# Two-layer attention kernel: the coarse score pieces of layer 0 by row halves of TensorE's array, and the softmax denominators as rows that VectorE inverts in PSUM

## The reference

```
layer 0:  theta, phi, g = W x + b       (64 rows each)
          f = softmax(theta^T phi);   y = f g;   x = W_out y + b_out + x
layer 1:  q, k, v = W x + b             (128 rows each)
          a = softmax(q^T k / sqrt(128));   x = x + v a^T
```

## Time and profile before

| | before |
|---|---|
| median of 3 runs | 3435.5 us |
| profiled execution, its own time | 3435.51 us |
| its span | 3433.7 us |
| granted clock, mean over the span | 0.989 |
| block of layer 0 (steady) | 44.03 us |
| block of layer 1 (steady) | 59.9 us |

### The profile page before, as it was taken

How to read it: one execution, slowest core, us unless ns; L and a number is a source line. 1 busy time by engine, 2 the same in 40 slices (tenths; PEclk the granted TensorE clock), 3 DMA queues, 4 the chain that set the end, 5 groups by cost and what they waited for, 6 DMA issues and landing times.

```text
span 3433.7 us, 46684 instructions
## 1 busy us (share of the span) xinstructions
PE 3336.5 (97%) x13124; PEld 2113.4 (62%) x13124; DVE 2100.6 (61%) x3029; ACT 1671.5 (49%) x2241; POOL 2965.9 (86%) x1366
## 2 busy tenths in 40 slices
PE   6999999999999989999999998999999999999998
PEld 4555566666655556666655555666665555566665
DVE  4555576776555557676755555677675555666674
ACT  4455445444455544444445554544454555444444
POOL 4999699898989969898989996989898999688897
PEclk9999999999999999999999999999999999999999
DMA  1000000000000000000000000000000000000000
GB/s 43 13 18 19 28 10 22 12 22 16 19 19 16 19 23 16 16 19 19 13 19 19 19 16 23 19 13 21 16 19 13 19 19 16 19 13 16 13 13 10
DMA packets 34038, 61.73 MB, mean 18 GB/s; under 512 B 5280, under 2 KB 5920, under 8 KB 33568
## 3 DMA queue, kind: packets, MB, share of 16 engines
q1 hardware_dynamic: 33824, 59.23, 5.6%
HBM read 42.44 MB, written 16.78 MB: 17 GB/s over the span
## 4 chain that ended last, share of the span: by engine, by line
PE 91%; DVE 3%; issue 2%; POOL 2%; ACT 1%; SPq 0%; DVEq 0%; DMA 0%; ACTq 0%; POOLq 0%
PE acc_out L471 16%; PE rough L398 15%; PE acc_out L455 13%; PE scores L420 7%; PE scores L423 7%; PE scores L425 7%; PE scores L429 7%; PE scores L426 7%; PE acc_out L443 2%; PE acc_out L441 2%; PE acc_out L442 2%; DVE piece_max L793 2%; PE rough L380 2%; PE acc_out L492 1%; PE acc_out L386 1%
## 5 line engine op out<-in xcount | busy, mean ns | idle before, releaser
L280 POOL TENSOR_TENSOR sums<-sums,probs 128x1024 f32<-128x1024 f32 x886 | 2116.0, 2388 | 145.1 <-ACT probs L718 104.7
L793 DVE TENSOR_REDUCE piece_max<-rough 128x1 f32<-128x512 f32 x2024 | 1309.5, 684 | 649.1 <-PE rough L398 646.2
L810 DVE TENSOR_TENSOR probs<-scores,shift_rows 128x1024 f32<-128x1024 f32 x512 | 626.7, 1224 | 567.3 <-PE scores L429 543.2
L718 ACT ACTIVATE probs<-scores 128x1024 f32<-128x1024 f32 x512 | 520.1, 1025 | 672.8 <-PE scores L423 665.1
L711 ACT ACTIVATE probs<-probs 128x1024 f32<-128x1024 f32 x512 | 539.4, 1053 | 499.6 <-DVE probs L810 499.4
L914 POOL TENSOR_TENSOR p_lo<-probs,p_hi 128x1024 fp32r<-128x1024 f32 x192 | 459.2, 2392 | 188.0 <-ACT probs L711 187.7
L471 PE MATMUL acc_out<-probs,v_vals 128*128 128x512 f32 x1280 | 605.4, 595 | 0.0
L425 PE MATMUL scores<-qry_a,k_hi 128*128 128x512 f32 x1024 | 507.8, 496 | 0.0
L455 PE MATMUL acc_out<-probs,g_vals 128*64 128x512 f32 x2048 | 495.0, 605 | 0.0
L420 PE MATMUL scores<-qry_a,phi_a 128*128 128x512 f32 x1024 | 432.3, 422 | 0.0
L710 ACT ACTIVATE p_hi<-probs 128x1024 fp32r<-128x1024 f32 x192 | 203.3, 1059 | 441.0 <-DVE probs L810 397.2
(11 more groups left out here) (97 smaller groups left out, 2961.0 us busy)
## 6 DMA issues: line engine op xcount, KB each, us to landing
x_q<-x SPq DMA_DIRECT2D x32, 256.0 KB, 2.7
x_res<-x SPq DMA_DIRECT2D x32, 256.0 KB, 3.0
mid<-mid_new SPq DMA_DIRECT2D x32, 256.0 KB, 2.2
x_q<-mid SPq DMA_DIRECT2D x32, 256.0 KB, 2.7
x_res<-mid SPq DMA_DIRECT2D x32, 256.0 KB, 3.2
out<-result SPq DMA_DIRECT2D x32, 256.0 KB, 2.3
x_kv<-x SPq DMA_DIRECT2D x24, 256.0 KB, 2.7
probs<-x SPq DMA_DIRECT2D x2, 1024.0 KB, 6.0
```

What stands on the lines that cost most here:

```text
L280: eng.tensor_tensor(sums[:, parity], sums[:, parity], probs[:, s % P_BUFS], ALU.add).then_inc(s_plus, 1)
L793: nc.vector.reduce_max(piece_max[:, t, c:c + 1], src, AX.X).then_inc(s_reduced, 1)
L810: nc.vector.tensor_tensor(probs[:, s % P_BUFS].rearrange("p (h c) -> p h c", c=QB), scores[:, s % 2].rearrange("p (h c) -> p h c", c=QB), ...
```

## The change

```diff
 DEN_AT = 5
-RDEN_AT = 8
+RECIP_AT = (6, 7, 8, 9)
+NORM_AT = 9
...
             def rough_piece(layer, parity, piece, place):
                 t, c = piece
-                keys = (phi_a, k_hi)[layer]
-                mm(place, qry_a[:, parity, t * P:(t + 1) * P], cols(keys, c), start=True, stop=True).then_inc(s_rough, 1)
+                at = slice(t * P, (t + 1) * P)
+                if layer == 1:
+                    mm(place, qry_a[:, parity, at], cols(k_hi, c), start=True, stop=True).then_inc(s_rough, 1)
+                elif t % 2 == 0:
+                    mm(place, qry_a[0:IC, parity, at], cols(phi_b, c)[0:IC], start=True, stop=True).then_inc(s_rough, 1)
+                else:
+                    mm(place, qry_a[IC:P, parity, at], cols(phi_a, c)[IC:P], start=True, stop=True).then_inc(s_rough, 1)
...
                 pe.wait_ge(s_y, g + 1)
                 pe.wait_ge(s_fold, g + 1)
-                for t in range(SUB):
-                    last = mm(acc_out[:, parity, 2 * t:2 * t + 2], total[:, t * P:(t + 1) * P], ones[:, 0:2],
-                              start=True, stop=True)
-                last.then_inc(s_den, 1)
-
-            def reciprocal_rows(g, parity):
-                pe.wait_ge(s_rdiag, 2 * g + 2)
-                mm(acc_out[:, parity], ones_r[:], rdiag[:, 0], start=True, stop=False)
-                mm(acc_out[:, parity], ones_r[:], rdiag[:, 1], start=False, stop=True).then_inc(s_rden, 1)
+                mm(acc_out[:, parity], ones[:], total[:], start=True, stop=True).then_inc(s_den, 1)
...
-                    if s == RDEN_AT and st.prev is not None:
-                        reciprocal_rows(st.g - 1, 1 - st.parity)
...
-                copy(cols(phi_b, c)[IC:P], src[IC:P], PHI_B[IC:P])
+                copy(cols(phi_b, c)[0:IC], src[0:IC], PHI_B[0:IC])
...
-                    copy(qry_b[0:IC, parity], acc_out[0:IC, parity]).then_inc(s_row_sb, 1)
+                    copy(qry_b[IC:P, parity], acc_out[IC:P, parity]).then_inc(s_row_sb, 1)
...
-            def reciprocal_diag(g, part):
-
-                act.wait_ge(s_rparts, 2 * g + part + 1)
-                for t in range(SUB):
-                    last = scaled(rdiag[:, part, t * P:(t + 1) * P], idt, rd(rparts[:, part, t:t + 1]))
-                last.then_inc(s_rdiag, 1)
...
-            def reciprocals(g, parity):
+            def reciprocal(g, parity, t):
+
                 dve.wait_ge(s_den, g + 2)
-                den = acc_out[:, parity, 0:2 * SUB].rearrange("p (t c) -> p t c", c=2)[:, :, 0:1]
-                rcol = acc_out[:, parity, 2 * SUB:3 * SUB]
-                nc.vector.reciprocal(rcol.unsqueeze(2), den).then_inc(s_rcol, 1)
-                dve.wait_ge(s_rcol, g + 1)
-                nc.vector.tensor_copy(rparts[:, 0], rcol).then_inc(s_rparts, 1)
-                dve.wait_ge(s_rparts, 2 * g + 1)
-                nc.vector.tensor_tensor(rparts[:, 1], rcol, rd(rparts[:, 0]), ALU.subtract).then_inc(s_rparts, 1)
+                at = acc_out[:, parity, t * P:(t + 1) * P]
+                nc.vector.reciprocal(at, at).then_inc(s_recip, 1)
...
-                        if s == DEN_AT + 1:
-                            reciprocals(g, parity)
-                        if s == RDEN_AT + 1:
+                        if s in RECIP_AT:
+                            reciprocal(g, parity, RECIP_AT.index(s))
+                        if s == NORM_AT:
                             normalise(layer, g, nth, parity)
...
-            nc.gpsimd.memset(phi_b[0:IC, :].bitcast(F32), 1.0 / IC).then_inc(s_ones, 1)
+            nc.gpsimd.memset(phi_b[IC:P, :].bitcast(F32), 1.0 / IC).then_inc(s_ones, 1)
+            pool.wait_ge(s_ones, 1)
```

More of the change, by code:

```diff
@@ L137, in build @@
         o_sb = sb("o_sb", [P, QB])
-        rparts = sb("rparts", [P, 2, SUB], F32R)
-        rdiag = sb("rdiag", [P, 2, QB], F32R)
         result = sb("result", [P, QB])
@@ L193, in build @@
         s_den = sem("s_den")
[L194 to L197, removed]
+        s_recip = sem("s_recip")
         s_wy = sem("s_wy")
@@ L619, in block_program @@
                     denominators(st.g, st.parity)
-                    reciprocal_rows(st.g, st.parity)
                     if st.layer == 0:
@@ L643, in copy @@
                 return nc.scalar.activation(dst, src, ACT.Identity, bias=bias, scale=scale)
-            def scaled(dst, src, scale):
-                return nc.scalar.activation(dst, src[:], ACT.Copy, scale=scale)
             def take_q_whole(g, layer, src):
@@ L751, in block_program @@
                         probs_shifted(st.g, st.nth, s)
-                    if s in (DEN_AT + 1, DEN_AT + 2) and st.prev is not None:
-                        reciprocal_diag(st.g - 1, s - DEN_AT - 1)
                     if st.phi_g:
@@ L773, in block_program @@
                     take_q_hi(1, st.parity, scores[:, 1, 0:QB])
-                if st.ends:
-                    reciprocal_diag(st.g, 0)
-                    reciprocal_diag(st.g, 1)
             def turn(b):
@@ L813, in shift_scores @@
                     shift_rows[:, parity].unsqueeze(1).to_broadcast([P, TPG, QB]), ALU.add).then_inc(s_shifted, 1)
-            def reciprocals(g, parity):
+            def reciprocal(g, parity, t):
                 dve.wait_ge(s_den, g + 2)
-                den = acc_out[:, parity, 0:2 * SUB].rearrange("p (t c) -> p t c", c=2)[:, :, 0:1]
-                rcol = acc_out[:, parity, 2 * SUB:3 * SUB]
-                nc.vector.reciprocal(rcol.unsqueeze(2), den).then_inc(s_rcol, 1)
-                dve.wait_ge(s_rcol, g + 1)
-                nc.vector.tensor_copy(rparts[:, 0], rcol).then_inc(s_rparts, 1)
-                dve.wait_ge(s_rparts, 2 * g + 1)
-                nc.vector.tensor_tensor(rparts[:, 1], rcol, rd(rparts[:, 0]), ALU.subtract).then_inc(s_rparts, 1)
+                at = acc_out[:, parity, t * P:(t + 1) * P]
+                nc.vector.reciprocal(at, at).then_inc(s_recip, 1)
             def normalise(layer, g, nth, parity):
-                dve.wait_ge(s_rden, g + 1)
+                dve.wait_ge(s_recip, SUB * g + SUB)
                 if layer == 0:
@@ L897, in block_program @@
                     fold(dve, st.g, st.parity)
-                    reciprocals(st.g, st.parity)
+                    for t in range(SUB):
+                        reciprocal(st.g, st.parity, t)
                     normalise(st.layer, st.g, st.nth, st.parity)
```

## The result

| | before | changed |
|---|---|---|
| median | 3434.99 us (4 runs) | 3469.3 us (4 runs, 3468.62 to 3473.07) |
| ratio | | 1.0108, 95% interval 1.0095 to 1.0121 |
| span of the profiled execution | 3433.7 us | 3466.5 us |
| steady block of layer 0 | 44.03 us | 45.0 us |
| block of layer 1 with / without the projection | 59.9 / 58.1 us | 60.05 / 58.8 us |

What follows compares the result with a forecast made beforehand. PE's queue was taken to bound both layers. Terms +31.9 (layer 0), +12.4 (mixed blocks), +15.9 (layer 1 inversions), -1.6 (last blocks) and +2.5 (ends) gave +61 on 3435.51, so 3497 us; range 3387 to 3560 us.

Steps and rivals of the forecast that it cites:

- Two changes of the array's shape cost more than a pair saves: PE, layer 0 pieces: each change to or from row halves costs 0.20 us; sum +1.3 us a block.
- Pairs run side by side: PE: two neighbouring pieces in row halves take 0.23 us instead of 0.46; 14 pairs a block, -3.2 us before shape changes.
- PE's saving by the denominators is eaten by waits: PE saves 0.41 us a block; waits for DVE's inversions make layer 1 +0.65 with the projection, +0.32 without.
- In the last image: Layer 1 blocks without the projection, 7 of them: +0.32 us each from waiting behind the inversions.
- The first block of layer 0 in images 1 to 3: Counted among the 28 layer 0 blocks that prepare layer 0, +1.14 us each.
- The ends: 5 ends, from L492 to the multiplication: 5.24 us becomes 5.7 with four inversions of 1.12, +2.5 together.
- The mixed blocks: 3 layer 1 blocks that prepare layer 0, all pieces between full matmuls: +4.1 us each, +12.4.
- The four rivals: Prediction's cases: slower as worked out (chance 0.50), faster (0.26), nearly no change (0.14), much slower (0.10).
- free changes of shape: Rival 2: going to row halves on PE costs nothing, so faster, -49 us to 3387 us; chance 0.26.
- half-price ones: Rival 3: a change of shape costs half of 0.20 us, so nearly no change, 3434 us; chance 0.14.
- halves that don't run side by side: Rival 4: row halves on PE don't run side by side, +100 us, 3597 us; chance 0.10.
- the inversions alone: Rival in e1_rows and e2_den: DVE's four inversions carry the slowdown, e2_den about 3465 us; no chance given.

Runs made afterwards that it cites:

- e1_rows: The kernel before with only the pieces of layer 0 in row halves, denominators as before: 3471.66 us, ratio 1.0114.
- e2_den: The changed kernel with layer 0's pieces as full matmuls again, so only the denominators changed: 3438.95 us, ratio 1.0016.
- e9_thirds_rows: e6_thirds with the pieces of layer 0 in row halves, as in the change: 3414.45 us, ratio 0.9955.
- e4_one_half: The changed kernel with all layer 0 pieces in the lower row half, so no two run side by side: 3550.04 us, ratio 1.034.
- e3_slots: e2_den with the same inversions moved into DVE's idle stretches, ahead of steps 6, 7 and 8: 3418.34 us, ratio 0.9957.
- e5_thirds_l1: e3_slots with layer 1's third pieces in steps 7, 10, 11, 13 instead of 7, 8, 10, 12: 3392.78 us, ratio 0.9886.
- e6_thirds: e5_thirds_l1 with layer 0's third pieces in steps 8, 10, 12, 13 instead of 7, 8, 11, 13: 3366.18 us, ratio 0.9811.
- e8_thirds_old_den: The kernel before with only the third pieces moved, to the steps used in e6_thirds: 3398.72 us, ratio 0.9907.

## Why the prediction was right, and where it was off

The forecast had 49 us for the row halves (28 x 1.3 and 12.4) and 12 for the denominators. Alone they measured 38 (e1_rows) and 5 (e2_den), and together 34. The sign and the main cost came as worked out; the sum was too high because the terms for a block of layer 0, for layer 1 and for the ends were all too large.

- **Two changes of the array's shape cost more than a pair saves: right.** 0.20 us per change, taken from the column halves, holds for row halves to 0.01 us (the rows above; +0.39 to +0.41 for a lone piece in e9_thirds_rows). In a block of layer 0, step 0 came at +0.18 (forecast +0.18), the third piece of 11 with the pair of 12 at +0.33 (+0.38), that of 13 at +0.15 (+0.20), and step 7 with the start of 8 at +0.17 (+0.2). The Trainium skill (TensorEngine Tiling (Array Packing), Key Properties) says that changing the tiling mode drains TensorE. The trace agrees for rows too, both ways: 0.32 us to the pair and 0.42 from it, where full matmuls start 0.23 apart. A term was missing: in step 14 PE had waited for a reduction ahead of the next queries, and that wait took up 0.17 us of the delay (0.21 in e9_thirds_rows). The steady blocks came at +0.90 us in the median, forecast +1.14: some 7 of the 27 us between forecast and result.
- **Pairs run side by side: right.** The starts show it, and e4_one_half gives its worth, 0.23 a pair between full matmuls.
- **PE's saving by the denominators is eaten by waits: right in sum, but in layer 1 largely by luck.** The inversions were mis-sized, 0.95 us instead of 1.21. The two short instructions gave 8.3 ns a column, and eight times a reduction's 1.0 seemed to bear it out; measured are 6.2. So nothing is lost in steps 6 and 7, and the projection comes 0.14 late, not 0.65. Layer 1 in images 0 to 2, put at 0.65 a block with the projection, came at 0.19. The waiting in step 8 was there before: the prediction took the 0.46 of the two matmuls as a saving that the inversions used up, while in layer 1 most of it had been filler in a wait for a reduction that the earlier trace rows show. e3_slots showed this, with the inversions out of the way and still no gain, and e5_thirds_l1 and e6_thirds against e8_thirds_old_den that the saving comes once the piece stands elsewhere.
- **In the last image** a block lost 0.64 us where 0.32 were forecast. (The 60.2 us that the prediction expected for a block without the projection took the length of one with it; such a block lasted 58.1 before and 58.8 now.) The delay shows in step 10 (+0.61), whose third piece waits for a reduction behind the fourth inversion, the multiplication, the finish and the shift. I had followed the delay only to step 8. With the fourth inversion in step 8 or earlier (e3_slots) that step is as before.
- **The first block of layer 0 in images 1 to 3** was put at the usual +1.14 and came at +1.9: it carries the same delay by the denominators of layer 1, 1.0 us in step 9 (e2_den has it too).
- **The ends**, with the last blocks of layer 0, were put at +0.9 us together and gave -4.8: four inversions back to back take 3.41 us, not 4.5. The pieces ahead of the first block are in row halves too; the prediction had no term for them, and the first scores come 2.3 us sooner (2.1 in e1_rows).
- **The mixed blocks** were put at +12.4 for the row halves alone. They came at 3.3 each in e1_rows, +9.9 together. In the change, with the inversions (0.5 each in e2_den), they came at 3.0.
- **Both parts together** cost 9 us less than the sum of the two. Most of it is step 8 of layer 0, where the two cover each other (under e2_den): 0.27 us a block, 28 blocks.

The four rivals: free changes of shape, and half-price ones, are ruled out by the starts; halves that don't run side by side are ruled out by e4_one_half. That the inversions alone are what makes it slower is ruled out by e2_den (+5 us), e1_rows (+38) and e9_thirds_rows.

Open is how much of the 0.09 us ahead of each first matmul of a new shape is emptying of the array: the starts give the time, and no run separates its cause.

## What to carry to other kernels

Before parts of the array are used side by side, count the changes of shape, not the matmuls: here each cost 0.2 us, nearly what a pair of 512-column fp32r matmuls saves (0.23), so even the best places only break even. Work taken off the limiting engine pays only where that engine does not wait for something else at that place: read what releases the next instruction before counting the saving. Long instructions on a helper engine (here four of 0.95 us a block) cost little in its idle stretches; spread one per step they cost 20 us more over the whole kernel (e2_den against e3_slots).

## What the runs showed of the hardware that was not expected

- RECIPROCAL on 128 partitions takes 182 ns for 4 columns and 953 ns for 128, 6.2 ns a column, six times the 1.0 of a reduction; two back to back take 1.77 us. The short instructions had pointed to 8.3 ns.
- A change between the full array and row halves costs about 0.09 us ahead of the first matmul and 0.11 us of exposed load (weights 128 columns wide), as the column halves had suggested. Within a pair the two matmuls start at the same time (238.32).
